# Block transposes on VectorE for three of sixteen attention units, whole mask columns, and two feature chunks kept in memory

## What is computed

```python
attn = jnp.einsum('nhc,mhc->hnm', q, k) / np.float32(np.sqrt(C))      # H, C = 4, 32
mask = adj == 0.0
neg = jnp.where(mask[None], -jnp.inf, attn)
m = jnp.max(neg, axis=-1, keepdims=True)
e = jnp.where(mask[None], 0.0, jnp.exp(neg - jnp.where(all_inf, 0.0, m)))
alpha = e / jnp.where(denom == 0.0, 1.0, denom)
out = jnp.einsum('hnm,mhc->hnc', alpha, v)
...
support_t = adj @ xt                                                   # fourth layer
```

## Time and profile before

| | |
|---|---|
| median of 3 runs | 1858.27 us (1858.11 to 1862.02) |
| profiled execution | 1859.99 us, its span 1858.3 us |
| TensorE busy | 1805.1 us (97%) |
| VectorE busy | 1229.1 us (66%) |
| ScalarE busy | 983.0 us (53%) |
| GpSimd busy | 925.3 us (50%) |
| moved by transfers | 328.82 MB, mean 177 GB/s |

### The profile page before, as it was taken

One profiled execution on the slowest core, in us unless ns is written; L12 is line 12 of the kernel. 1 busy time (PEld: TensorE's weight loads), 2 busy tenths in 40 slices (PEclk: granted clock), 3 DMA queues, 4 the chain that ended last, 5 costly groups with the idle time before them and its releaser, 6 DMA issues.

```text
span 1858.3 us, 41304 instructions
## 1 busy us (share of the span) xinstructions
PE 1805.1 (97%) x15504; PEld 1215.9 (65%) x15504; DVE 1229.1 (66%) x2398; ACT 983.0 (53%) x1512; POOL 925.3 (50%) x981
## 2 busy tenths in 40 slices
PE   7999999999996999999999999999999999999996
PEld 3444444444444888888888888888888888644442
DVE  4777775122226888898888888888988889401322
ACT  0111110101004888888888888988888988501101
POOL 0111111111225756778788788787787886540211
PEclk9999999999997999999999999999999999999998
DMA  9867767799977322213222222232133231697781
GB/s 376 303 227 260 256 225 251 270 391 380 400 271 220 93 91 72 83 58 95 88 73 90 74 82 86 70 92 91 60 93 93 64 96 49 242 356 281 281 325 71
DMA packets 110305, 328.82 MB, mean 177 GB/s; under 512 B 13104, under 2 KB 31280, under 8 KB 85552
## 3 DMA queue, kind: packets, MB, share of 16 engines
q1 hardware_dynamic: 87552, 285.25, 43.9%
q10 hardware_dynamic: 20016, 32.78, 4.9%
q0 software_dynamic: 2560, 8.39, 1.6%
HBM read 299.11 MB, written 27.26 MB: 176 GB/s over the span
## 4 chain that ended last, share of the span: by engine, by line
PE 59%; issue 3%; ACT 2%; POOL 2%; DVE 1%; POOLq 0%; DVEq 0%; ACTq 0%
PE bank L580 21%; PE bank L553 13%; PE bank L594 13%; PE bank L446 11%; ACT arena L807 2%; POOL arena L1360 1%; DVE arena L1124 1%; PE bank L434 0%; ACT L858 0%; PE bank L622 0%; PE bank L690 0%; POOL small L1480 0%; ACT arena L819 0%; PE bank L602 0%; POOL small L1367 0%
## 5 line engine op out<-in xcount | busy, mean ns | idle before, releaser
L580 PE MATMUL bank<-ident,arena 128*128 128x128 f32 x4096 | 540.0, 274 | 5.4 <-ACT arena L807 2.4
L580 PEld LDWEIGHTS bank<-ident,arena 128*128 128x128 f32 x4096 | 478.1, 141 | 82.5 <-DVE arena L1124 7.7
L807 ACT ACTIVATE arena<-arena,small 128x2048 f32<-128x2048 f32 x256 | 512.5, 2002 | 0.1
L819 ACT ACTIVATE arena<-bank 128x512 f32<-128x512 f32 x680 | 382.4, 596 | 125.3 <-PE bank L580 123.0
L446 PE MATMUL bank<-arena,stat_s 128*128 128x512 f32 x1008 | 441.4, 595 | 2.1 <-issue 1.2
L553 PE MATMUL bank<-k,parts 128*128 128x512 f32 x1024 | 371.8, 445 | 13.3 <-DVE small L1109 7.0
L446 PEld LDWEIGHTS bank<-arena,stat_s 128*128 128x128 f32 x1008 | 190.2, 191 | 228.3 <-issue 226.9
L1124 DVE COPY arena<-bank 128x512 f32<-128x512 f32 x344 | 236.7, 688 | 73.3 <-PE bank L580 71.6
L1360 POOL TENSOR_SCALAR early<-arena 128x512 bf16<-128x512 f32 x128 | 246.3, 1925 | 68.9 <-DVE small L1109 26.7
L594 PE MATMUL bank<-arena,stat_x 128*32 128x128 f32 x8192 | 276.5, 276 | 0.0
L1360 POOL TENSOR_SCALAR arena<-arena 128x512 bf16<-128x512 f32 x128 | 247.2, 1931 | 40.5 <-DVE small L1109 19.8
(11 more groups left out here) (152 smaller groups left out, 1182.8 us busy)
## 6 DMA issues: line engine op xcount, KB each, us to landing
arena<-adj_cols SPq DMA_DIRECT2D x190, 1024.0 KB, 6.3
arena<-adj SPq DMA_DIRECT2D x256, 256.0 KB, 2.7
k_dram<-arena ACTq DMA_DIRECT2D x32, 256.0 KB, 6.7
q_dram<-arena ACTq DMA_DIRECT2D x32, 256.0 KB, 11.7
k<-k_dram POOLq DMA_DIRECT2D x32, 256.0 KB, 8.5
parts<-q_dram SPq DMA_DIRECT2D x128, 64.0 KB, 2.3
x_dram<-arena ACTq DMA_DIRECT2D x16, 256.0 KB, 3.6
arena<-x_dram ACTq DMA_DIRECT2D x16, 256.0 KB, 4.9
```

The costliest lines, as they stand in the source:

```text
L580: last = pe.transpose(bank[:, b_, h * P:(h + 1) * P], cols[:, st % SETS, h, u * P:(u + 1) * P], ident[:, :])
L807: act.activation(cols[:, s_, h, :], cols[:, s_, h, :], ACT.Exp, bias=shift[:, t % 2, 1, i:i + 1], scale=-1.0, accum_out=blocksum[:, t % 2, ...
L819: act.activation(turned[k % TURNED], bank[:, TURN_BANKS.bank(("unit", k)), :], ACT.Copy).then_inc(unit_copied_act, 1)
```

## The change

Of the 16 units of a set, three (places 7, 14 and 15, `BLOCK_TURN_AT`) are no longer turned by TensorE. VectorE turns them in blocks of 32x32 straight from `cols` into `group_blocks`, the last 8 tiles of `stat_s`, at places 0, 5 and 7 of the set. A block transpose leaves each 32x32 block at its old place among the partitions; to put the blocks where they belong the data goes through memory: SP stores a group (unit 7 alone, 256 KB; units 14 and 15 together, 512 KB) in one transfer and loads it back in four transfers of 32 partitions, into the buffers 6 and 7 of `turned`. There are no copies out of a bank for these units. TensorE waits for `group_landed` ahead of their products and reads them with a strided pattern.

The copies that are left are dealt anew: 20 of 104 in a chunk by VectorE, 84 by ScalarE; the places of most exponentials move by one to four. The mask inputs are whole columns of 1024 in two buffers (the second lies in the tiles of `stat_s` for chunks 4 and 5), so that GpSimd converts a column with one instruction, and SP loads them 7 columns ahead of the place. Because that buffer occupies their tiles, the features of chunks 4 and 5 are stored to memory at the start of chunks 6 and 7 (GpSimd's step at its slot 4 waits for that) and loaded back after the attention (`load_xt`). The loads of residuals move to the end of a chunk.

```diff
-VECTOR_PLACES = (2, 5, 9, 12, 15)
-VECTOR_ALSO = (38, 58, 84, 87, 91, 93)
+BLOCK_TURN_AT = {7: 0, 14: 5, 15: 7}
+GROUPS = ((7,), (14, 15))
+VECTOR_PLACES = ()
+VECTOR_ALSO = (1, 9, 16, 27, 29, 34, 48, 51, 58, 67, 74, 81, 83, 84, 89, 92, 96, 107, 115, 122)
+MASK_AHEAD = 7
+SPILLED = (4, 5)
...
+        group_slots = arena[:, RING + 10 * CHUNK:RING + 12 * CHUNK]
+        group_blocks = stat_s[:, TILES - 2 * TPC:TILES, :].rearrange("p t f -> p (t f)")
+        spilled = stat_s[:, SPILLED[0] * TPC:(SPILLED[-1] + 1) * TPC, :].rearrange("p t f -> p (t f)")
+        adj_in = (arena[:, RING + 4 * CHUNK:RING + 6 * CHUNK], spilled)
...
+            def store_group(g):
+                i, n = groups_until(g), len(group_of(g))
+                sp.wait_ge(blocks_turned, block_turns(g + n))
+                if i >= 2:
+                    sp.wait_ge(group_landed, 16 * (P // C) * (i - 1))
+                sp.dma_start(group_dram[i % 2, :, 0:n * CHUNK], group_blocks[:, 0:n * CHUNK]).then_inc(group_out, 16)
+            def load_group(g):
+                i, n = groups_until(g), len(group_of(g))
+                slots = slots_of(group_of(g))
+                sp.wait_ge(group_out, 16 * (i + 1))
...
+                if g + n > TURNED:
+                    sp.wait_ge(unit_used, g + n - TURNED)
+                for j in range(P // C):
+                    sp.dma_start(slots[j * C:(j + 1) * C, :].rearrange("k (q n) -> k q n", q=P // C),
+                                 group_dram[i % 2, :, j * n * P:(j + 1) * n * P].rearrange("(q k) n -> k q n", q=P // C)
+                                 ).then_inc(group_landed, 16)
+            def attention_loads(c):
+                for st in range(SPC):
+                    for half_set in range(2):
+                        groups = [group for group in GROUPS if group[0] // UPB == half_set]
+                        ahead = c * COLS + 2 * st + half_set + MASK_AHEAD
+                        if half_set == 1:
+                            for group in groups:
+                                store_group(c * UPC + st * UPS + group[0])
+                        if ahead < CHUNKS * COLS:
+                            load_mask(ahead // COLS, ahead % COLS, False)
+                        if half_set == 0:
+                            for group in groups:
+                                store_group(c * UPC + st * UPS + group[0])
...
+                        for group in groups:
+                            load_group(c * UPC + st * UPS + group[0])
+                load_residuals(c)
...
-                if k in BY_VECTOR:
+                if is_block_turned(k):
+                    pe.wait_ge(group_landed, 16 * (P // C) * (groups_until(c * UPC + k) + 1))
+                elif k in BY_VECTOR:
...
-                    turn_unit(c, k, first)
+                    if not is_block_turned(k):
+                        turn_unit(c, k, first)
...
-                        dve.wait_ge(unit_turned, (c * COLS + m - 3) * UPB)
+                        dve.wait_ge(unit_turned, pe_turns((c * COLS + m - 3) * UPB))
+                        dve.wait_ge(blocks_turned, block_turns((c * COLS + m - 3) * UPB))
...
+            def turn_blocks(c, k):
+                st, u = k // UPS, k % UPS
+                i = groups_until(c * UPC + k)
+                dve.wait_ge(exp_ready, (c * SPC + st) * H + H)
+                if i > 0:
+                    dve.wait_ge(group_out, 16 * i)
+                n = len(group_of(k))
+                dve.transpose(group_tiles(group_blocks[:, 0:n * CHUNK], n)[:, in_group(k), :, :, :],
+                              cols[:, st % SETS, :, u * P:(u + 1) * P].rearrange("p h (j k) -> p h j k", j=P // C)
+                              ).then_inc(blocks_turned, 1)
...
-                for e in range(2):
-                    pool.wait_ge(adj_landed[e], 16 * (c * COLS + m + 1))
-                    pool.nop(nofuse=True)
-                    pool.tensor_scalar(maskbias[m % 4][:, e * HALF:(e + 1) * HALF], adj_in[e], 0.0, MASKED,
-                                       ALU.is_equal, ALU.mult).then_inc(bias_ready, 1)
+                pool.wait_ge(adj_landed[m % 2], 16 * ((c * COLS + m) // 2 + 1))
+                pool.nop(nofuse=True)
+                pool.tensor_scalar(maskbias[m % 4], adj_in[m % 2], 0.0, MASKED, ALU.is_equal,
+                                   ALU.mult).then_inc(bias_ready, 1)
```

More of the change, by code:

```diff
@@ L100, in __call__, with is_block_turned, pe_turns, groups_until @@
         return c * len(self.names) + self.names.index(name) + 1
+def is_block_turned(k):
+    return k % UPS in BLOCK_TURN_AT
+PE_UNITS = [k for k in range(UPC) if not is_block_turned(k)]
+def pe_turns(g):
+    return g // UPC * len(PE_UNITS) + sum(k < g % UPC for k in PE_UNITS)
+def groups_until(g):
+    return g // UPS * len(GROUPS) + sum(group[-1] < g % UPS for group in GROUPS)
+def block_turns(g):
+    return g // UPS * len(BLOCK_TURN_AT) + sum(u < g % UPS for u in BLOCK_TURN_AT)
+def group_of(k):
+    return [group for group in GROUPS if k % UPS in group][0]
+def in_group(k):
+    return group_of(k).index(k % UPS)
 class TurnBanks:
@@ L141 @@
 LAST_BLOCK_CHUNK = CHUNKS - BLOCK // CHUNK
-BY_VECTOR = [k for k in range(UPC) if (k % 16 in VECTOR_PLACES or k in VECTOR_ALSO) and k not in VECTOR_NOT]
-BY_SCALAR = [k for k in range(UPC) if k not in BY_VECTOR]
+BY_VECTOR = [k for k in PE_UNITS if (k % 16 in VECTOR_PLACES or k in VECTOR_ALSO) and k not in VECTOR_NOT]
+BY_SCALAR = [k for k in PE_UNITS if k not in BY_VECTOR]
 EXP_PLACES = [EXP_MOVED.get(k, k) for k in range(1, UPC, 4)]
@@ L356, in load_queries @@
                                  ).then_inc(q4_landed[t % 2], 16)
-            def attention_loads(c, first):
-                for m in range(COLS):
-                    if m % BLOCKS == 0:
-                        load_queries(c, m // BLOCKS, first)
-                    if not (first and m == 0):
-                        load_mask(c, m, first)
-                    if m == 5 and not first:
-                        load_residuals(c - 1)
-                    if m == 15 and not first:
-                        store_x3(c - 1)
@@ new lines, in store_xt, with load_xt @@
+            def store_xt(c):
+                sp.wait_ge(att_pool, AG(c, "xt"))
+                sp.dma_start(xt_dram[c - SPILLED[0], :, :], mx_g).then_inc(xt_out, 16)
+            def load_xt():
+                sp.wait_ge(bias_ready, CHUNKS * COLS)
+                for i in range(len(SPILLED)):
+                    sp.wait_ge(xt_out, 16 * (i + 1))
+                    sp.dma_start(spilled[:, i * CHUNK:(i + 1) * CHUNK], xt_dram[i, :, :]).then_inc(xt_in_place, 16)
+            def load_residuals(c):
+                if c == 0:
+                    sp.wait_ge(gcn_q_out, 64 * CHUNKS)
+                    sp.wait_ge(gcn_root_out, 16 * CHUNKS)
+                    sp.wait_ge(gcn_x2_out, 16 * CHUNKS)
+                else:
@@ L1211, in attention @@
                         below_max(c, k // UPT)
+                    for u, place in BLOCK_TURN_AT.items():
+                        if k % UPS == place:
+                            turn_blocks(c, k - place + u)
                     if k in BY_VECTOR:
```

96 lines of the change are left out of this document (59 added, 37 removed).

## The result

The changed kernel takes 1853.24 us (median of 10 runs, 1847.97 to 1856.07) against 1858.78 us for the kernel before on the same chip (10 runs, 1857.85 to 1862.63). The ratio is 0.9955 [0.994, 0.997]: 0.45% faster. 1795 us had been forecast, with a range from 1768 to 1840: of the 64 us of gain some 6 came, and the time lies outside the range. The profiled execution took 1850.57 us for a span of 1848.9 us.

A forecast was written before the change was run, and what follows sets the result against it. TensorE was taken to bound the attention at 16.0 us a set, VectorE and ScalarE close behind; 1858.3 - 70 (64 sets at 14.9 us) + 6 at the end = 1794 us of span, so 1795 us, range 1768 to 1840.

The forecast's parts named there:

- The price of the turn: VectorE in the attention: a block transpose of 512 numbers a partition takes 0.69 us, with bounds 0.53 and 1.59 us.
- both rivals of a dear turn: VectorE's block transpose: at 1.1 us 1843 us (chance 0.09); over 1.21 us slower, up to 1934 us (0.08, shared with late trip).
- The set of 14.9 us: Attention: a set falls from 16.0 to 14.9 us, between bounds 14.55 and 15.5 us; 70 us gained over 64 sets.
- The price of a turned unit: TensorE in the attention: turning costs 0.48 us a unit; three units fewer leave 14.55 us of work a set.
- The strided reading: TensorE's products of the block-turned units: costed at nothing; at a tenth of 0.25 us it would be 0.08 us a set.
- The start: Start of the attention: TensorE's last key load wait (6.30 us, until 590.13) stays; later mask loads hide behind it: 0.
- SP's queue: Mask column and query loads ahead of the group loads cost nothing; if late, 1.86 us of issuing.
- place 5 of VectorE: Turn of unit 14 waits for unit 7's store, 4.4 us against 4.7; 1 us later, VectorE stands 0.7 us a set.
- the sign of being wrong: Profile after: wrong if transposes take over 1 us, group load waits stand in every set, or VectorE stands before place 5's turn.
- the round trip rival: From place 7 to the pair's landing: binds over 11.7 us; at 12.1 us the set is 15.5 us, kernel 1832 us.
- Round trip or the place 5 wait late, but a gain: Outcome in the attention: the trip's landing or VectorE's place 5 wait is late, yet the kernel gains; chance 0.14.
- The end: First product of the fourth layer: TensorE waits some 6 us for the first slot, bounds 2 and 10 us, the last pair's wait inside.

The follow-up runs named there:

- without the trip: Changed kernel without the stores and loads of turned groups; TensorE multiplies straight from the staging buffers (another result): 1799.24 us, 0.9675 of the kernel before.
- the end loads: Changed kernel with group stores ahead of mask loads, plus last residual and feature loads moved ahead of the last half set: 1827.42 us, 0.982 of the kernel before.
- groups first: Changed kernel with each group's store and loads both ahead of the mask load, in both halves of a set: 1849.56 us, 0.9936 of the kernel before.

## Why the prediction was wrong, step by step

**The price of the turn: right.** 0.69 us was taken, 706 ns measured, 0.02 us off. By the Trainium skill's figure ("VectorE: DVE Perf Modes", "The three transpose paths") the estimate was 1.24 us for the 512 numbers; the measurement decides, and both rivals of a dear turn fall. VectorE is busy 747.5 / 53.7 = 13.9 us a set without the trip (14.21 forecast).

**The set of 14.9 us: right, but in part by luck.** It came out in the kernel without the trip, whose 1799 us are 4 us from the forecast. Its two terms did not come out. TensorE is busy 789.0 / 53.5 = 14.75 us a set there, and idle for 0.21 us; 14.55 us of work and 0.35 us of waiting were forecast. The price of a turned unit, 0.48 us, was read at the end of the attention, where no scores stand between the earlier trace rows. Among scores it is less, as a stretch of sixteen units, with the same small step for a tile's end in it and without a stall, shows. Before, between two batches of products:

```profile
1005.75 1.08 PE L594 MATMUL bank<-arena,stat_x 128*32 128x128 f32 x32
...
1021.50 1.08 PE L594 MATMUL bank<-arena,stat_x 128*32 128x128 f32 x32
```

In the change, between two turns of the same place of a set:

```profile
1005.55 0.60 PE L674 MATMUL bank<-ident,arena 128*128 128x128 f32 x4
...
1020.12 0.60 PE L674 MATMUL bank<-ident,arena 128*128 128x128 f32 x4
```

That is 15.75 us before (with three turns more) and 14.57 us in the change: 1.18 us saved, 0.39 us a unit. So TensorE's own gain was forecast some 0.09 x 3 x 64 = 17 us too high, and the waiting of the engines on each other by most of that too high as well, which hid it. The strided reading costs nothing: 32 matmuls of the products take 1.08 us in both.

**The start: right.** TensorE waits until 590.54 for the key load (590.13 before).

**SP's queue: the step that failed.** The prediction said: "On SP, ahead of the group loads, stand the mask column and every second set four query loads; both are issued while SP would wait for the store anyway, so they cost nothing". I had priced the mask load's issue and not the wait ahead of it, on GpSimd's conversion, and in the first half of the set the mask stands ahead of the store as well as of the loads. The place where it would show was named (place 5 of VectorE, "if that store takes 1 us more"), and so was the sign of being wrong that came, VectorE standing ahead of the turn there; but the 4.4 us against 4.7 us had no term for standing in the queue, and the store was priced at 3.7 us, where it took 4.1 us behind a 512 KB mask (2.6 us ahead of it). What the runs showed in place of "nothing": SP stands 82.3 us in 800 for the conversions ahead of mask loads, VectorE 36.8 us behind it, and store and mask in the other order take 24 us off the kernel, the queries behind the loads a further 11 us. "If they were late it would be 1.86 us of issuing" was wrong too: late, the mask load cost its wait, up to 6.5 us.

**The size of the round trip rival.** "Round trip or the place 5 wait late, but a gain" had a chance of 0.14, and the rival a time of 1832 us, 37 us over the forecast; it came to 58 us over it. What came is for the most part the wait at place 5 (TensorE waits 22.6 us in 800 for masks behind it) and to a lesser one the late landing that the rival describes (14.1 us). The rival's set of 15.5 us is near: idle time alone would make it 14.9 + 0.64 = 15.5 us. What it lacked is mostly the clock. Busy time a set is 757.0 / 50.75 = 14.92 us in the change (203 exponentials stand in the window, four a set) and 789.0 / 53.5 = 14.75 us without the trip: 0.17 us a set or 11 us in all that TensorE works longer for the same instructions, at a granted clock down to 0.50 after a stall. (The 6.3 us that the rival's text takes for a queue with mask columns in front are the landing times of the other layers' 1 MB slots, with no mask among them.)

**The end: mechanism right, size short.** 6 us were forecast. The timeline there:

```profile
1591.33 1.52 PE L696 MATMUL bank<-arena,stat_x 128*32 128x128 f32 x48
...
1595.15 4.60 SPq L383 DMA_DIRECT2D arena<-adj_cols  x8
1596.58 1.08 PE L696 MATMUL bank<-arena,stat_x 128*32 128x128 f32 x16 [3.74 <-DMA arena<-group_dram]
1602.15 4.61 PE L540 MATMUL bank<-arena,stat_s 128*128 128x512 f32 x5 [4.49 <-DMA arena<-adj_cols]
```

TensorE stands 3.74 us for the last pair and then 4.49 us for the slot, 8.2 us in all. The pair's wait does lie in the slot's, as forecast: had the pair landed at once, TensorE would have stood all of it for the slot, and the end loads show it (8.1 us in all in other shares). What was short is the time from the last group's loads to the slot's landing, 1590.66 to 1602.15, 11.5 us, where the bytes alone gave 8 us: the first slot is issued only 4.5 us after them. The 8 first products of the fourth layer then take 5.99 us (3.70 before), at a granted clock of 0.50 from 1602 to 1606 (1.00 before). How much of the end is the trip's own no run separates: without the trip TensorE stands 5.92 us for the slot as well, but that kernel's feature loads wait for products of the last set.

**Where the 58 us went.** The account is a rough one, from one profiled execution of each kernel. Idle time of TensorE a set is 43.0 / 50.75 = 0.85 us in the change and 11.0 / 53.5 = 0.21 us without the trip: 0.64 x 64 = 41 us. The lower clock is 11 us, the end 8.2 - 5.9 = 2.3 us more than without the trip, and without the trip the kernel is 4 us over the forecast. Sum 58 us. By cause, in the order in which the kernels take them away: from 1853 to 1829 us the order of store and mask (24 us); to 1819 us the queries ahead of the pair's loads (11 us); to 1816 us the single staging buffer (3 us, not certain); from there to 1805 us, by difference alone, TensorE's remaining waits for landings (11 us), the last pair's at the end among them; to 1799 us the bytes (5 us, not certain).

**Left open.** That the conversion ahead of the longest stand is late because of GpSimd's steps is read from the timeline. Whether GpSimd's conversions could be brought forward at the end of a chunk, ahead of its L1483 steps, which would remove the cause of the queue's longest stand, was not tried. How much of the 11 us of clock belongs to which stall is not known.

## What to carry to other kernels

SP works off its transfers in order (the store of unit 7, turned by 1204.86, went out at 1209.79, just behind the mask load of 1209.34), so a load that waits for a buffer to come free holds up every store and load behind it: for each transfer of a critical round trip, list the waits of all that stands ahead of it, not only their issue times. A prefetch with a tight buffer can cost as much as the trip (groups first lost 20 us), so neither order is right throughout; here the store had to go first, then the mask, then the group's loads, then the queries. And when a wait is cured by one more buffer without touching what is late, look for the consumer that gets it next.

## What the runs showed of the hardware

VectorE's transpose of 128x512 four-byte numbers in blocks of 32x32 takes 706 ns, next to 683 to 688 ns for a copy of as many. After a 5.1 us stand of TensorE the granted clock was 0.50 from 1218 to 1220 and 0.72 from 1220 to 1222, and 1.00 again from 1222 on, so that a short stall costs more than itself: eight transposes took 1.91 us there instead of 1.04. Doubling the transfer traffic, in as many transfers as the trips have, cost 5.5 us of 1800, not clear of the spread, where TensorE did not wait for it. The four loads of 32 partitions landed in 2.1 us at 64 KB each and 3.5 us at 128 KB; the prediction took 2.3 us from the query loads for the smaller. The Trainium skill ("SBUF — State Buffer", "Summary: rules for kernel authors") asks for one transfer over all 128 partitions; no run here has a trip of that form, so what the four cost against one is not known. And 512 KB loads issued from GpSimd's queue instead of SP's made the kernel 49 us slower (1878 against 1829 us).
